# A causal convolution of four taps written as three convolutions of two taps over half the columns

## The chip, the cores and the metric

The kernel runs on one core of one Trainium2 chip. The metric is the device time in microseconds from the first to the last instruction of that core. The engines are named as in the profile: PE is TensorE, DVE is VectorE, ACT is ScalarE, POOL is GpSimd and SP is SyncE, which here only issues DMAs. PSUM is the memory that PE writes, in eight banks of 512 float32 columns.

## The reference

A state-space block and a feed-forward block with selected tokens, each followed by a layer norm. The input is `x`, four batches of 512 tokens of 256 channels, all float32. The first block, cut to what matters here:

```python
xz = x @ W_in
xc, r = jnp.split(xz, 2, axis=-1)
xt = xc.transpose(0, 2, 1)
xconv = lax.conv_general_dilated(xt, conv_w, (1,), [(3, 0)])     # 4 taps, 256 -> 256 channels, causal
xs = (xconv + conv_b[None, :, None]).transpose(0, 2, 1)
u = silu(xs)
dbc = u @ W_x
delta = softplus(dbc[..., :dtr] @ W_dt + b_dt)                   # then B and C from dbc
# scan over 512 tokens: h = exp(delta * A) * h + delta * u * B;  y = sum over 16 states of h * C
out = (y + u * D) * silu(r)
return out @ W_out + xs                                          # x + this goes into the layer norm
```

The second block picks 64 tokens of each batch by a router score, runs attention and a gated MLP over these 256 tokens, puts them back, and a last layer norm follows.

## The kernel before

Channels lie on the 128 partitions (two halves, `o` or `i` = 0, 1) and the 512 tokens of one batch along the free dimension. `W_in` is multiplied into the taps at the start, on PE, so that the convolution reads `x` itself: `conv_x[k, i]` holds the weights of tap k for input half i. `xT` is the transposed `x` of one batch with three zero columns (`PAD`) ahead.

Each engine has a program written out by hand; they meet only in semaphores. The work of a batch is cut into pieces, and the lists `FRONT_AT` (L42), `TAIL_AT` (L53), `FIRST_FRONT` (L49) and `EARLY` (L51) say at which step each engine issues its part of a piece. The main loop has 64 steps t, 16 for each batch b, each with two scans:

- DVE: `scan(2t)`, `scan(2t+1)` (L1179), each over 128 x 512, which write `state`; then its parts of the pieces of step t.
- PE: `turn_bu(2t+2)`, `add_states(t-3)`, the tail pieces, `turn_bu(2t+3)`, the front pieces. `turn_bu(u)` (L651) transposes a quarter of `zed` into the bank that scan u reads, four banks in turn, so it waits for scan u-4. `add_states` (L668) folds the weighed states into a bank.
- ACT: `make_decay(2t+2)`, `make_decay(2t+3)` (L1030; each needs scan u-4 done), in even steps six instructions of `make_z` (L1016), then tail and front pieces.
- POOL: `weigh(t-1)` (L1557), the rest of `make_z`, and other pieces.

Pieces of batch b run ahead of its scans: `xT0`, `xT1` (PE transposes, ACT copies them out of PSUM into `xT`) at step 16b-24, the convolution quarters `cv0a` to `cv0d` at 16b-23 to 16b-20 and `cv1a` to `cv1d` at 16b-19 to 16b-16, `su` (ACT: silu of the convolution) at 16b-13. For batch 2 these are steps 8, 9 to 16 and 19, for batch 3 steps 24, 25 to 32 and 35. Batch 0 does all of them ahead of the loop. Batch 1 does `xT` to `cv1a` ahead of the loop (list `EARLY`, with `du0`, `du1` of batch 0 after `cv0b`, `turn_bu(0)` after `cv0c`, `turn_bu(1)` after `cv0d`), and `cv1b` to `cv1d` at steps 0 to 2.

`convolve(b, o, quarter)` (L542) is one quarter of the convolution for output half o: two matmuls of 128 x 128 weights over 512 columns. Eight of them, for four taps and two input halves, add up in one bank. In the trace a float32 matmul of the program is two MATMUL records. When the last quarter is filled, ACT copies the bank with the bias added into `xsT` (L929).

The front pieces share PSUM banks 6 and 7 in turn: `add_rest` (L115) gives them out in the order of the program, and a convolution holds its bank from `cv?a` to `cv?d` (`held`). `wait_free(pe, name)` makes PE wait until the bank's last contents are drained.

In the list ahead of the loop, DVE is free until the softplus of batch 0 (piece `s3`, L1199), whose two halves end in `delta` and `duT`; SP then spreads `delta` by eight DMAs for the first decays. In steps 10 and 11 DVE has `s4`, `s5` and `s6` of batch 1 (L1217, L1224, L1229); for later batches POOL does `s5` and `s6`.

## Time and profile before

| | us |
|---|---|
| median of three runs | 477.36 (476.84 to 479.91) |
| the profiled execution | 478.12 |
| its span, first to last instruction | 476.4 |

The profile is one execution. Spans and starts below are microseconds from its first instruction. Engines work side by side, so a change is worth what the engine that others wait for gains at that place. The first scan starts at about 61 us and the last step of the loop ends at about 335 us; all that is changed lies between 20 and 211 us.

### The profile page before, as it was taken

Reading aid. Unit: us, or ns where it says so; the run is one execution under the profiler, and the core shown is the slowest. Engines: PE = TensorE matmul, PEld = TensorE weight load, DVE = VectorE, ACT = ScalarE, POOL = GpSimd, SP = SyncE. Lnnn points to the kernel's source line nnn. Section 1 sums busy time; section 2 is a strip of 40 time slices with the busy share of each in tenths; the row PEclk is TensorE's granted clock in tenths of the full one; section 3 lists DMA queues with packets and bytes.
Section 4 is the critical chain, followed back from the end, with each engine's and each line's share of the span. In section 5 each row is a group of like instructions: output and inputs, shape, how many; then the busy total and the mean of one; then the engine's idle time right before and its main releaser. Section 6 shows DMA issues by size and latency. Waiting matters only on the chain. (4 is left out here: it accounts for less than half of the span.)

```text
span 476.4 us, 6481 instructions
## 1 busy us (share of the span) xinstructions
PE 413.1 (87%) x2037; PEld 250.5 (53%) x2037; DVE 302.2 (63%) x604; ACT 294.5 (62%) x628; POOL 278.7 (59%) x245
## 2 busy tenths in 40 slices
PE   4997899889999989999978789768978998999991
PEld 3442453344446435545434456333666877888880
DVE  0400665479683568965659977999488596554355
ACT  4325688796777795678699576963262556543152
POOL 2001056859888859979778999977653254331022
PEclk9998999999999979999988899979997999999996
DMA  6100611004310000510000514870400000000013
GB/s 231 48 6 14 164 48 45 22 23 97 106 45 23 21 23 14 142 46 24 23 22 3 124 55 146 274 287 2 178 0 2 0 1 1 3 1 0 1 53 123
DMA packets 18710, 29.10 MB, mean 61 GB/s; under 512 B 2699, under 2 KB 10677, under 8 KB 18421
## 3 DMA queue, kind: packets, MB, share of 16 engines
q1 hardware_dynamic: 18676, 28.70, 19.4%
q8 instruction: 16, 0.26, 0.2%
q14 instruction: 18, 0.14, 0.1%
HBM read 22.27 MB, written 2.23 MB: 51 GB/s over the span
## 5 line engine op out<-in xcount | busy, mean ns | idle before, releaser
L1186 DVE TENSOR_TENSOR_SCAN state<-front_a,bank 128x512 f32<-128x512 f32 x88 | 102.9, 1206 | 43.8 <-PE bank L538 22.0
L538 PEld LDWEIGHTS bank<-ident,loop_buf 128*128 128x128 f32 x512 | 60.4, 146 | 82.1 <-issue 37.7
L538 PE MATMUL bank<-ident,loop_buf 128*128 128x128 f32 x512 | 85.0, 291 | 16.2 <-ACT loop_buf L1027 14.6
L1037 ACT ACTIVATE front_a<-loop_buf,a_neg 128x512 f32<-128x512 f32 x128 | 84.2, 711 | 7.8 <-DVE copy L1186 4.6
L1027 ACT ACTIVATE loop_buf<-copy,b_rows 128x256 f32<-128x256 f32 x190 | 78.9, 495 | 0.1
L554 PE MATMUL bank<-front_c,conv_raw 128*128 128x512 f32 x128 | 60.7, 607 | 2.5 <-ACT front_c L902 0.9
L1186 DVE TENSOR_TENSOR_SCAN copy<-front_a,bank 128x512 f32<-128x512 f32 x40 | 47.0, 1208 | 23.5 <-PE bank L538 8.1
L1563 POOL TENSOR_TENSOR state<-state,front_a 128x1024 f32<-128x1024 f32 x22 | 52.5, 2387 | 6.1 <-DVE state L1186 6.0
L1563 POOL TENSOR_TENSOR state<-state,c_own 128x1024 f32<-128x1024 f32 x22 | 52.7, 2396 | 4.2 <-DVE state L1186 3.9
L675 PE MATMUL bank<-state,fold 128*64 128x512 f32 x176 | 51.2, 661 | 0.8 <-POOL state L1563 0.8
L1576 POOL TENSOR_TENSOR loop_buf<-copy,b_rows 128x512 f32<-128x512 f32 x31 | 33.6, 1084 | 24.5 <-ACT copy L902 21.9
L554 PEld LDWEIGHTS bank<-front_c,conv_raw 128*128 128x128 f32 x128 | 23.0, 195 | 22.9 <-issue 20.8
L1592 POOL TENSOR_TENSOR loop_buf<-state 128x256 f32<-128x256 f32 x24 | 17.9, 746 | 27.2 <-DVE state L1332 27.2
L1536 POOL TENSOR_TENSOR copy<-front_c,front_b 128x1024 f32<-128x1024 f32 x4 | 8.0, 2003 | 38.0 <-ACT front_b L902 33.1
L902 ACT ACTIVATE front_b<-bank,vec 128x512 f32<-128x512 f32 x16 | 10.9, 683 | 29.4 <-PE bank L554 26.3
L902 ACT ACTIVATE copy<-bank 128x512 f32<-128x512 f32 x20 | 11.7, 595 | 25.7 <-PE bank L538 15.6
L1563 POOL TENSOR_TENSOR copy<-copy,front_a 128x1024 f32<-128x1024 f32 x10 | 24.6, 2465 | 2.7 <-DVE copy L1186 2.7
L699 PE MATMUL bank<-h,copy 128*128 128x128 f32 x192 | 24.4, 283 | 1.4 <-ACT h L1044 0.9
L1563 POOL TENSOR_TENSOR copy<-copy,c_own 128x1024 f32<-128x1024 f32 x10 | 23.9, 2391 | 2.6 <-DVE copy L1186 2.6
L699 PEld LDWEIGHTS bank<-h,copy 128*128 128x128 f32 x192 | 23.0, 196 | 4.3 <-issue 3.0
L675 PE MATMUL bank<-copy,fold 128*64 128x512 f32 x80 | 22.5, 641 | 0.4 <-POOL copy L1563 0.4
L1204 DVE TENSOR_SCALAR front_c<-front_b 128x512 f32<-128x512 f32 x2 | 0.9, 430 | 30.3 <-ACT front_b L966 30.3
(202 smaller groups left out, 740.1 us busy)
## 6 DMA issues: line engine op xcount, KB each, us to landing
front_a<-c_stage SPq DMA_DIRECT2D x32, 128.0 KB, 2.9
c_own<-c_stage SPq DMA_DIRECT2D x32, 128.0 KB, 2.8
loop_buf<-front_b SPq DMA_DIRECT2D x32, 128.0 KB, 2.3
copy<-in_L_attn_x SPq DMA_DIRECT2D x4, 512.0 KB, 3.8
front_b<-in_L_ffn_wo SPq DMA_DIRECT2D x1, 2048.0 KB, 10.9
copy<-in_L_ffn_wq SPq DMA_DIRECT2D x1, 2048.0 KB, 8.0
out<-loop_buf SPq DMA_DIRECT2D x3, 512.0 KB, 3.0
conv_raw<-in_L_attn_conv_w SPq DMA_DIRECT2D x2, 512.0 KB, 4.2
```

Source lines behind the costliest of these rows:

```text
L538: return pe.transpose(dst, src, ident[:])
L554: mm = pe.matmul(at(name)[:], conv_x[:, k, i, o * P:(o + 1) * P], xT[:, i, k:k + L], start=(j == 0), stop=(j == TAPS * KD - 1))
L675: mm = pe.matmul(bank[Y_BANK[h]][j * P // 2:(j + 1) * P // 2, :], fold[:], state[t % NH][:, j, :], start=(m == 0), stop=(m == NPAIR - 1))
L699: mm = pe.matmul(at(name)[:, i * P:(i + 1) * P], w_qk[:, k, head * P:(head + 1) * P], hT[:, k, p * P:(p + 1) * P], start=(k == 0), stop=(k ...
L902: drain_done(name, act.activation(dst, at(name)[:] if src is None else src, func, **kw))
L1027: act.activation(zed[:, g % NZ, c, :, i, :], du_rows[b % 2][:, c, :].rearrange("p (k d) -> p k d", k=2 * KD), ACT.Copy, scale=b_rows[:, b ...
L1037: act.activation(decay[:, u % NDA, :], delta_wide[:, b % 2, k, :], ACT.Exp, scale=a_neg[:, k, m:m + 1]).then_inc(decay_made, 1)
L1186: dve.tensor_tensor_scan(state[t % NH][:, j, :], decay[:, u % NDA, :], bank[BU_BANK[u % NBU]][:], 0.0, ALU.mult, ALU.add).then_inc(scanned, 1)
L1536: pool.tensor_tensor(resT[b % 2], xT[:, :, PAD:], xsT, ALU.add).then_inc(res_ready, 1)
L1563: pool.tensor_tensor(state[t % NH], state[t % NH], c_wide[g % NCW].unsqueeze(1).to_broadcast([P, 2, L]), ALU.mult).then_inc(weighed, 1)
L1576: pool.tensor_tensor(zed[:, g % NZ, c], rows, cols, ALU.mult).then_inc(z_pool, 1)
L1592: pool.tensor_tensor(qkT[:, 2 * j:2 * j + 2, p * P:(p + 1) * P], qk_raw[:, i0 % NQK], qk_swap[:, i0 % NQK], ALU.add).then_inc(roped, 1)
```

## The change

The four-tap convolution of one output half becomes three parts, each of two taps over every second column. With even outputs y0 and odd outputs y1, A = the even taps over the even shifts, B = the odd taps over the odd shifts, S = the sums of neighbouring taps over the sums of neighbouring columns:

- part a (`even0`, `even1`): four matmuls of 257 columns, `conv_x[0]` and `conv_x[2]` over `xT` read with a step of two elements, into a bank of its own. ACT copies it out into `even_buf`.
- part b: four matmuls of 256 columns, taps 1 and 3, again with a step of two, into the first half of the bank of `cv0` or `cv1`.
- part c: four matmuls of 256 or 255 columns, `tap_sum` over `x_pair`, into the second half of that bank.
- part d: nothing on PE. DVE puts the outputs together in three instructions.

DVE also makes `x_pair` from the bank of `xT0` and `xT1`, after ACT has copied from it, and the bank is free only then. DVE makes `tap_sum` once. The bank of even0 comes out of the same turn as the others. ACT no longer copies the convolution out, and at the start of the loop it has `cv1a` of batch 1 where it had `cv0d`. `even_buf` and `odd_part` lie in the buffer of `gT`, `tap_sum` in that of `h`, `x_pair` in that of `change`.

```diff
             if piece[:2] == "cv":
                 if piece[-1] == "a":
+                    add_rest(("even" + piece[2], b))
+                elif piece[-1] == "b":
                     held[0] = add_rest((piece[:3], b))
...
-            def convolve(b, o, quarter):
-
-                name = (f"cv{o}", b)
-                if quarter == 0:
+            def convolve(b, o, part):
+
+                out = slice(o * P, (o + 1) * P)
+                wait_drained(pe, ("xT0", b))
+                wait_drained(pe, ("xT1", b))
+                if part == "a":
+                    name = (f"even{o}", b)
                     wait_free(pe, name)
...
+                        mm = pe.matmul(at(name)[:, 0:HALF + 1], conv_x[:, 2 * m, i, out], xT[:, i, 2 * m:2 * m + L + 1:2],
+                                       start=(j == 0), stop=(j == 2 * KD - 1))
+                    fill_done(name, mm)
+                elif part == "b":
+                    name = (f"cv{o}", b)
+                    wait_free(pe, name)
...
+                        mm = pe.matmul(at(name)[:, 0:HALF], conv_x[:, 2 * m + 1, i, out], xT[:, i, 2 * m + 1:2 * m + L:2],
+                                       start=(j == 0), stop=(j == 2 * KD - 1))
+                elif part == "c":
+                    name = (f"cv{o}", b)
                     if b == 0:
...
+                        pe.wait_ge(taps_added, 4)
+                    for i in range(KD):
+                        mm = pe.matmul(at(name)[:, HALF:], tap_sum[:, 1, i, out], x_pair[:, i, :],
+                                       start=(i == 0), stop=(i == KD - 1), skip_group_check=True)
+                    for i in range(KD):
+                        mm = pe.matmul(at(name)[:, HALF + 1:], tap_sum[:, 0, i, out], x_pair[:, i, 0:HALF - 1],
+                                       start=False, stop=True, skip_group_check=True)
                     fill_done(name, mm)
...
-                    copy_out(name, xT[:, o, PAD:])
+                    wait_filled(act, name)
+                    act.activation(xT[:, o, PAD:], at(name)[:], ACT.Copy).then_inc(x_copied, 1)
...
-                elif piece in ("cv0d", "cv1d"):
+                elif piece in ("cv0a", "cv1a"):
...
-                    copy_out((piece[:3], b), xsT[:, o, :], func=ACT.Identity, bias=vec[:, CB + o:CB + o + 1])
+                        wait_drained(act, (f"cv{o}", b - 1))
+                    copy_out((f"even{o}", b), even_buf[:, o, :], at((f"even{o}", b))[:, 0:HALF + 1])
...
+            front(1, "cv0a")
             front(0, "du0")
             front(0, "du1")
             make_z(0, 0)
...
             make_decay(0)
             make_decay(1)
-            front(1, "cv0d")
+            front(1, "cv1a")
...
+            def add_taps():
+
+                for v in range(4):
+                    j, k = v // 2, 2 * (v % 2)
+                    wait_drained(dve, ("vc", v))
+                    dve.tensor_tensor(tap_sum[:, k // 2, j, :], conv_x[:, k, j, :], conv_x[:, k + 1, j, :],
+                                      ALU.add).then_inc(taps_added, 1)
+
             def front(b, piece):
-                if piece == "s3" and b == 0:
+                if piece in ("xT0", "xT1"):
+                    o = int(piece[-1])
+                    dve.wait_ge(x_copied, KD * b + o + 1)
+                    drain_done((piece, b), dve.tensor_reduce(x_pair[:, o, :], at((piece, b))[:].rearrange("p (s e) -> p s e", e=2),
+                                                             AX.X, ALU.add))
+                elif piece in ("cv0d", "cv1d"):
+                    o = int(piece[2])
+                    name, t = (f"cv{o}", b), at((f"cv{o}", b))
+                    wait_drained(dve, (f"even{o}", b))
+                    wait_filled(dve, name)
...
+                    dve.scalar_tensor_tensor(out=cols[:, 0], in0=t[:, 0:HALF], scalar=shift_by, in1=even_buf[:, o, 0:HALF],
+                                             op0=ALU.add, op1=ALU.add)
+                    link(dve.tensor_tensor(odd_part, t[:, 0:HALF], even_buf[:, o, 1:], ALU.add))
+                    drain_done(name, dve.scalar_tensor_tensor(out=cols[:, 1], in0=t[:, HALF:], scalar=shift_by, in1=odd_part,
+                                                              op0=ALU.add, op1=ALU.subtract))
...
+                    for piece in ("xT0", "xT1"):
+                        front(1, piece)
                     for h in range(KD):
                         dve.wait_ge(sp_log, h + 1)
...
+            add_taps()
             for piece in FIRST_FRONT:
                 front(0, piece)
...
                 scan(2 * t)
                 scan(2 * t + 1)
+                if t == 0:
+                    front(1, "cv0d")
```

## Rows read from the trace of the kernel before

**Rows 1.** The page, busy time of each engine, share of the span, instructions.

```profile
PE 413.1 (87%) x2037; PEld 250.5 (53%) x2037; DVE 302.2 (63%) x604; ACT 294.5 (62%) x628; POOL 278.7 (59%) x245
```

**Rows 2.** Timeline (start, duration, instructions, idle before), ahead of the loop.

```profile
21.12 0.60 ACT L902 ACTIVATE front_c<-bank 128x512 f32<-128x512 f32 x1 [0.26 <-PE bank L538]
21.92 13.97 PE L554 MATMUL bank<-front_c,conv_raw 128*128 128x512 f32 x32 [0.84 <-issue]
35.93 0.69 ACT L902 ACTIVATE front_b<-bank,vec 128x512 f32<-128x512 f32 x1 [3.47 <-PE bank L554]
36.65 1.06 ACT L938 ACTIVATE copy<-front_b 128x1024 f32<-128x1024 f32 x1
37.85 3.65 PE L582 MATMUL bank<-copy,w_x_s 128*128 128x512 f32 x4 [1.96 <-ACT copy L938]
```

**Rows 3.** Timeline of PE: one quarter in steps 12 and 25, and 257-column matmuls.

```profile
114.38 1.88 PE L554 MATMUL bank<-front_c,conv_raw 128*128 128x512 f32 x4
174.84 3.41 PE L554 MATMUL bank<-front_c,conv_raw 128*128 128x512 f32 x4
201.90 1.90 PE L641 MATMUL bank<-x,onehot 128*64 128x257 f32 x8
```

**Rows 4.** Groups of PE instructions: transposes (busy us, mean ns | idle before).

```profile
L538 PE MATMUL bank<-ident,conv_raw 128*128 128x128 f32 x16 | 3.9, 424 | 4.4 <-DMA conv_raw<-in_L_attn_conv_w 4.4
L538 PE MATMUL bank<-ident,front_a 128*128 128x128 f32 x4 | 1.1, 428 | 1.0 <-DMA front_a<-in_L_attn_W_in 1.0
```

**Rows 5.** Groups of DVE instructions of 256 and 128 columns.

```profile
L1388 DVE TENSOR_REDUCE top<-bank 128x1 f32<-128x256 f32 x16 | 6.6, 415 | 0.0
L1387 DVE TENSOR_REDUCE top<-bank 128x1 f32<-128x128 f32 x16 | 4.7, 291 | 13.8 <-PE bank L799 13.7
L1439 DVE SCALAR_TENSOR_TENSOR change<-bank,gate,state 128x256 f32<-128x256 f32 x2 | 1.0, 484 | 5.2 <-PE bank L859 5.2
L1402 DVE TENSOR_TENSOR state<-bank,sel 128x256 f32<-128x256 f32 x2 | 0.8, 424 | 3.2 <-PE bank L827 3.2
```

**Rows 6.** Groups of ACT instructions: the bias copy, and a copy of 257 columns.

```profile
L902 ACT ACTIVATE front_b<-bank,vec 128x512 f32<-128x512 f32 x16 | 10.9, 683 | 29.4 <-PE bank L554 26.3 <-PE bank L602 3.1
L1010 ACT ACTIVATE sel<-bank 64x257 f32<-64x257 f32 x4 | 1.5, 381 | 14.8 <-PE bank L641 14.8
```

**Rows 7.** Timeline from the softplus of batch 0 to step 3.

```profile
52.33 3.67 PE L554 MATMUL bank<-front_c,conv_raw 128*128 128x512 f32 x8 [0.94 <-ACT front_c L902]
52.70 0.69 DVE L1210 TENSOR_TENSOR front_b<-front_b 128x512 f32<-128x512 f32 x1 [0.55 <-ACT front_b L977]
60.24 1.33 ACT L1037 ACTIVATE front_a<-loop_buf,a_neg 128x512 f32<-128x512 f32 x2 [0.89 <-DMA loop_buf<-front_b]
61.07 2.36 DVE L1186 TENSOR_TENSOR_SCAN state<-front_a,bank 128x512 f32<-128x512 f32 x2 [1.44 <-ACT front_a L1037]
62.12 0.69 ACT L902 ACTIVATE front_b<-bank,vec 128x512 f32<-128x512 f32 x1 [0.54 <-PE bank L554]
72.72 0.69 ACT L902 ACTIVATE front_b<-bank,vec 128x512 f32<-128x512 f32 x1 [1.45 <-PE bank L554]
```

**Rows 8.** Timeline of steps 8 to 14: DVE from the scans of step 8, and ACT.

```profile
94.96 2.33 DVE L1186 TENSOR_TENSOR_SCAN state<-front_a,bank 128x512 f32<-128x512 f32 x2 [3.35 <-issue]
98.28 2.33 DVE L1186 TENSOR_TENSOR_SCAN state<-front_a,bank 128x512 f32<-128x512 f32 x2 [0.99 <-PE bank L538]
101.11 1.05 ACT L902 ACTIVATE front_c<-bank 128x512 f32<-128x512 f32 x2
108.78 3.12 DVE L1224 TENSOR_TENSOR front_b<-front_b 128x1024 f32<-128x1024 f32 x1
115.11 6.76 DVE L1186 TENSOR_TENSOR_SCAN state<-front_a,bank 128x512 f32<-128x512 f32 x6
```

**Rows 9.** Timeline of steps 24 to 32: the same places one batch later.

```profile
168.44 2.33 DVE L1186 TENSOR_TENSOR_SCAN state<-front_a,bank 128x512 f32<-128x512 f32 x2 [0.99 <-PE bank L538]
173.22 1.06 ACT L902 ACTIVATE front_c<-bank 128x512 f32<-128x512 f32 x2
```

More of the change, by code:

```diff
@@ L316, in block_kernel @@
         gT = gT_buf[:].rearrange("p (k l) -> p k l", k=KD)
+        HALF = L // 2
+        even_buf = gT_buf[:, 0:KD * (HALF + 1)].rearrange("p (k s) -> p k s", k=KD)
+        odd_part = gT_buf[:, KD * (HALF + 1):KD * (HALF + 1) + HALF]
         z = sb("z", [P, C, DM])
@@ L333, in block_kernel @@
         sel = sb("sel", [P, ST, NCOL])
+        tap_sum = h_buf[:].rearrange("p (m k o) -> p m k o", m=TAPS // 2, k=KD)
+        x_pair = change_buf[:].rearrange("p (k s) -> p k s", k=KD)
         cosT = sb("cosT", [P, S])
@@ L380, in block_kernel @@
         pool_seq = sem("pool_seq")
+        x_copied = sem("x_copied")
+        taps_added = sem("taps_added")
         u_ready = sem("u_ready")
@@ L549, in convolve @@
                     pe.wait_ge(conv_pad, 1)
-                for j in range(2 * quarter, 2 * quarter + 2):
-                    k, i = j // KD, j % KD
-                    if b == 0:
-                        wait_drained(pe, ("vc", 2 * i + k // 2))
-                    mm = pe.matmul(at(name)[:], conv_x[:, k, i, o * P:(o + 1) * P], xT[:, i, k:k + L],
-                                   start=(j == 0), stop=(j == TAPS * KD - 1))
-                if quarter == 3:
+                    for j in range(2 * KD):
+                        m, i = j // KD, j % KD
+                        if b == 0:
+                            wait_drained(pe, ("vc", 2 * i + m))
+                        mm = pe.matmul(at(name)[:, 0:HALF + 1], conv_x[:, 2 * m, i, out], xT[:, i, 2 * m:2 * m + L + 1:2],
+                                       start=(j == 0), stop=(j == 2 * KD - 1))
@@ new lines, in convolve @@
+                    fill_done(name, mm)
+                elif part == "b":
+                    name = (f"cv{o}", b)
+                    wait_free(pe, name)
+                    for j in range(2 * KD):
+                        m, i = j // KD, j % KD
+                        mm = pe.matmul(at(name)[:, 0:HALF], conv_x[:, 2 * m + 1, i, out], xT[:, i, 2 * m + 1:2 * m + L:2],
+                                       start=(j == 0), stop=(j == 2 * KD - 1))
+                elif part == "c":
+                    name = (f"cv{o}", b)
+                    if b == 0:
+                        pe.wait_ge(taps_added, 4)
[5 more added lines that the diff above has]
+                                       start=False, stop=True, skip_group_check=True)
@@ L922, in front @@
                         act.preload_act_table_set("natural_log_exp_and_others")
-                elif piece in ("cv0d", "cv1d"):
+                elif piece in ("cv0a", "cv1a"):
                     o = int(piece[2])
-                    if b == 0 and o == 0:
-                        wait_drained(act, "vec")
                     if b >= 1:
-                        act.wait_ge(res_ready, b)
-                    copy_out((piece[:3], b), xsT[:, o, :], func=ACT.Identity, bias=vec[:, CB + o:CB + o + 1])
+                        wait_drained(act, (f"cv{o}", b - 1))
+                    copy_out((f"even{o}", b), even_buf[:, o, :], at((f"even{o}", b))[:, 0:HALF + 1])
                     if b == 0 and o == 0:
@@ L934, in front @@
                 elif piece == "su":
+                    wait_drained(act, ("cv0", b))
                     wait_drained(act, ("cv1", b))
@@ L1196, in make_z @@
                                       ALU.mult).then_inc(z_dve, 1)
-            def front(b, piece):
-                if piece == "s3" and b == 0:
+            def add_taps():
[4 more added lines that the diff above has]
+                                      ALU.add).then_inc(taps_added, 1)
+            def front(b, piece):
+                if piece in ("xT0", "xT1"):
[8 more added lines that the diff above has]
+                    wait_filled(dve, name)
+                    if b == 0 and o == 0:
+                        wait_drained(dve, "vec")
+                    if b >= 1:
+                        dve.wait_ge(res_ready, b)
+                        dve.wait_ge(u_ready, b)
+                    cols = xsT[:, o, :].rearrange("p (s e) -> p e s", e=2)
+                    shift_by = vec[:, CB + o:CB + o + 1]
+                    dve.scalar_tensor_tensor(out=cols[:, 0], in0=t[:, 0:HALF], scalar=shift_by, in1=even_buf[:, o, 0:HALF],
[3 more added lines that the diff above has]
+                                                              op0=ALU.add, op1=ALU.subtract))
+                elif piece == "s3" and b == 0:
                     for h in range(KD):
```

4 lines of the change are left out of this document (1 added, 3 removed).

## The prediction

> **What bounds the kernel now.** I read the page's busy times first. PE is busy for 87% of the span, DVE, ACT and POOL for about 60% each [rows 1]. That makes PE the engine to relieve, but it is an average, so I then read the timeline of each engine at the places where the change lies. Ahead of the loop PE works alone: ACT sits idle for 3.47 us until the convolution's last matmul, and the silu follows directly [rows 2]. In the loop the four engines run in a ring: PE's transposes wait for the scan four back, a decay waits for the scan four back, a scan waits for both. Whoever is last in a step sets it. During convolution steps this is mostly PE, but at the start of the loop and around `xT` it is ACT (DVE waited 1.44 us for a decay [rows 7]) or the order of DVE's list.
>
> **What PE loses.** In the program's float32 a quarter is four records of 512 columns: 1.88 us, with the end of the last one, or 13.97/8 = 1.75 us in a row of eight [rows 2, 3]. Eight records of 257 columns took 1.90 us [rows 3], so a part a, b or c costs what a quarter did. Three in place of four take 1.75 us from each of eight half-convolutions: 14 us of PE's work, 3.5 per batch.
>
> Parts a and b read every second column. No row shows whether that costs anything. Lower bound nothing; upper bound twice the time, 1.75 us more for each part. The nearest rows are transposes out of `conv_raw` with a step of four elements in one of the two operands, 424 ns each, beside 428 ns for those with a step of one [rows 4]: equal. I take nothing. The Trainium skill (SBUF — State Buffer, Door 1: The DMA port swizzle) says that SBUF is read in lines of 16 bytes and that a second access to the same line comes at full rate, which for float32 with a step of two would be free. By the same rule a step of four should cost something; the two rows differ by nothing, though they do not tell which operand has the step. The sum is the same by page and rows.
>
> **What DVE gains.** A reduce of 256 columns takes 415 ns and one of 128 takes 291 [rows 5], 0.97 ns a column, so 512 columns are 0.66 us; per batch two, 1.3 us. The three instructions of part d read PSUM and SBUF over 256 columns: 484, 424 and 484 ns [rows 5], 1.4 us per half. DVE gets 4.1 us per batch. The four `tap_sum` adds (about 0.42 each) run while PE still makes the taps, and part c needs them only 3.5 us after the convolution starts: nothing. ACT changes a 683 ns copy for one of 381 [rows 6], 0.6 us less per batch, and no longer waits for the last quarter. Bounds of DVE's share: 0.3 us a half less (if the instructions overlap their ends) to 0.7 us more (beside POOL, where L1224 took 3.12 us for 1024 columns [rows 8]; those two inputs both lie in SBUF, the new ones don't).
>
> **Ahead of the loop.** PE starts when both banks of `xT` are free: ACT's copy ends at 21.72, the reduce at about 22.4, so +0.5. Two quarters less: -3.5. The output is put together in 1.4 us on DVE instead of 0.69 on ACT: +0.7. The silu comes 2.3 us early, at 34.3. PE then waits as before, and its four records of 3.65 us after the pause of 1.96 (0.9 us each instead of 0.44: the lower clock [rows 2]) stay.
>
> **Into the loop.** In `s3` DVE has the two reduces between its two halves. Before the add at 52.70 it had 0.55 us to spare [rows 7], so 1.3 - 0.55 = +0.75, and the decays and the first scan come 1.5 us early, at 59.5. The convolution of batch 1 waited for ACT's copy until 52.33; now it waits for the second reduce.
>
> Now the step that I take as decisive. Counting `add_rest` through the new list puts cv0 of batch 1 in bank 6, du0 in 7 and even1 again in bank 6. So PE's `cv1a` waits until DVE has drained cv0, and DVE does this after both scans of step 0: 59.5 + 2.3 + 1.4 = 63.2. Queued behind `cv1a` on PE are `turn_bu(2)` and (3); behind even1's copy on ACT are decays 2 and 3, so DVE's next scans. Part a ends at 65.0, the copy at 65.5. Before, ACT's copy at this place ended at 62.8 [rows 7]: +2.7. ACT then worked on to its next copy at 72.72, ahead of which it was idle for 1.45 us [rows 7]. The idle time and the copy itself (0.6) are gone, so at step 3 ACT is 0.7 us later than before: the 1.5 us gained are lost and 0.7 more. PE has stood idle for 4 us ahead of part a. After 1.96 us it fell to the lower level [rows 2], and a quarter at that level took 3.41 instead of 1.88 [rows 3]. I expect that here too: +1.6. Sum to step 3: **+2.3** (bounds +0.7 and +2.5; -1.5 if the wait is hidden).
>
> **Batch 2, steps 8 to 17.** DVE is done with step 8 at 97.3, but its reduces stand ahead of step 9 and need ACT's copies, which come at 101.11 to 102.16, after a decay pair and `make_z` [rows 8]. Step 9 scans at 103.0 instead of 98.28: 4.7 us late. From 98.28 to L1224 at 108.78 DVE had three pairs of scans and `s4`, 8.2 of 10.5 us, so 2.3 are absorbed and 2.4 remain. Then `cv0d` adds 1.4 after step 12: the scans that ended at 121.9 [rows 8] end at 125.7. PE loses its quarter at 114.38, but must then wait for the first scan of step 12, to about 118.8: this quarter is traded for idle time. In steps 14 to 16 PE sets the pace again and its missing last quarter gives 1.75 back, against 1.4 for `cv1d` on DVE. ACT, no longer waiting for cv1d, comes to `su` up to 1 us early. That is -1.0 to 0; the 4 us pause of PE adds up to 1.5 by the clock. I take **+0.5**.
>
> **Batch 3, steps 24 to 33.** The same with ACT's copies at 173.22 to 174.3 [rows 9], since `la0` and `la1` stand ahead of them: step 25 scans at 175.1 instead of 168.44, +6.7. PE had its `cv0a` only at 174.84 [rows 3], so it loses just 0.3; POOL has its own waits there. DVE catches up to about +3.3 at step 30, with `cv0d` in it, and two quarters less bring PE back: at step 34 the scans stand at +0.2, ACT at -1 or better, and ACT sets the next steps. **-1.0** (bounds -1.7 and +3.3).
>
> **Sum.** 2.3 + 0.5 - 1.0 = +1.8 us, so the execution of 478.12 becomes 479.9. It lies 0.76 above the median of 477.36; against the median the forecast is 479.2 us, +0.4%. Of 14 us taken from PE nearly all goes into waits. [...]
>
> **The rivals.** *PE's time comes through*, 20%: batch 1's wait is hidden and half of the six quarters in the loop reach the end: -1.5 - 5.2 = -6.7, 470.7 us. For it: PE is busy 87%, and it is idle for little in the convolution steps. Against it: DVE's list around `xT`. *DVE's delays are never given back*, slower, 19%: a scan waits for ACT's `xT` copy with all of DVE behind it. It decides once DVE stays the last engine through steps 14 and 30: +2.3 + 3.8 + 3.3 = +9.4, 486.8 us. Against it: PE is idle then and has less to do. *The step of two costs PE double*, 4%: 7 us more per batch, all of it ahead of the loop and half of it in three batches: +1.8 + 7 + 10.5 = +19, 497 us. Against it: rows 4.
>
> **How the numbers follow.** My forecast has 57% and by its bounds (-1.0, +0.7 and up to +3) runs from 475 to 483. The range reaches from 471 to 487, beyond which lie half of the faster rival, the double read and some of the slow one, together 2 in 10. This kernel's measurement tells about 1%, 4.8 us, from no change. Faster than 472.6: 0.18. Slower than 482.1: 0.26, the slow rivals and the upper end of mine. Between: 0.56.
>
> **What the changed profile would show.** Ahead of the loop: 48 records of 257, 256 and 255 columns about 10.5 us long, silu near 34.3; 17 us or more if the step of two costs. First scan near 59.5. PE idle for about 4 us ahead of the first record of even1, with DVE as releaser, and a lower clock after it; ACT's decay pair after it near 66 to 67. DVE idle from 97 to 102 until ACT's copy, with the scans of step 9 behind it, and from 167 to 174. PE idle for some 4 us near 115. I am wrong in the main step if PE is not idle ahead of even1, and in the sum if step 17 and step 34 begin over 2 us away from where these terms put them.

## The result, and the profile after

The changed kernel took 485.28 us (median of 4 runs, 484.31 to 491.5), the kernel before 478.02 beside it on the same chip (4 runs): a ratio of 1.0168, 95% interval 1.0118 to 1.0218. It is 1.7% slower. The time lies in the range of 471 to 487, but the forecast of 479.2 was 6 us too low. "Within 1%", which had the largest chance, did not come, and the time lies outside the 475 to 483 that the prediction gave to its own case. (Ratios leave out executions in which the chip was disturbed, the medians and ranges here don't, so the two can differ by some tenths of a per cent.)

| | before | after |
|---|---|---|
| median | 478.02 us | 485.28 us |
| profiled execution, its time | 478.12 us | 484.31 us |
| its span | 476.4 us | 482.6 us |
| mean granted clock of TensorE in it | 0.952 | 0.942 |

The page of after, busy times (compare [rows 1]):

```profile
PE 405.5 (84%) x2101; PEld 267.1 (55%) x2101; DVE 316.9 (66%) x640; ACT 292.8 (61%) x628; POOL 278.7 (58%) x245
```

PE is busy 7.6 us less and the span is 6.2 us longer: PE stands idle for about 14 us more than before. Where it does, the groups of lines tell (busy us, mean ns | idle time before them and what ended it); L564 is part a, L1238 the reduce, L1252 to L1255 part d:

```profile
L564 PE MATMUL bank<-front_c,conv_raw 128*128 128x257 f32 x64 | 20.8, 478 | 13.7 <-DVE change L1238 5.4 <-DVE junk L1327 4.8 <-DVE front_b L1255 3.4
L1238 DVE TENSOR_REDUCE change<-bank 128x256 f32<-128x512 f32 x8 | 5.2, 688 | 11.1 <-ACT front_c L941 11.0
L1252 DVE SCALAR_TENSOR_TENSOR front_b<-bank,vec,gT 128x256 f32<-128x256 f32 x8 | 3.8, 473 | 11.0 <-PE bank L582 11.0
L1254 DVE TENSOR_TENSOR gT<-bank,gT 128x256 f32<-128x256 f32 x8 | 3.3, 412 | 0.0
L1255 DVE SCALAR_TENSOR_TENSOR front_b<-bank,vec,gT 128x256 f32<-128x256 f32 x8 | 3.9, 484 | 0.3
```

Of PE's 14 us of new idle time most stands ahead of one line, part a (the convolution's line of before had 2.5 us ahead of it), and each of its three releasers is DVE: 5.4 us for the sums of neighbours, 3.4 us for the bank of `cv0` of batch 1, and 4.8 us for "junk L1327", which the prediction does not mention. DVE itself waits 11.0 us for ACT's copies ahead of the reduces.

The timeline of after ahead of the loop (start, duration, instructions, idle before; compare [rows 2]):

```profile
21.76 2.05 PE L564 MATMUL bank<-front_c,conv_raw 128*128 128x257 f32 x8 [1.46 <-DVE change L1238]
23.65 1.98 PE L572 MATMUL bank<-front_c,conv_raw 128*128 128x256 f32 x8
34.26 1.06 ACT L965 ACTIVATE copy<-front_b 128x1024 f32<-128x1024 f32 x1 [4.67 <-DVE front_b L1255]
35.46 1.95 PE L609 MATMUL bank<-copy,w_x_s 128*128 128x512 f32 x4 [2.74 <-ACT copy L965]
```

The silu starts at 34.26, 2.4 us earlier than before. The four records behind it took 1.95 us, where before they took 3.65, though PE had stood idle for longer (2.74 us, not 1.96).

The way into the loop (compare [rows 7]):

```profile
51.84 3.13 PE L572 MATMUL bank<-front_c,conv_raw 128*128 128x256 f32 x8
59.03 2.33 DVE L1214 TENSOR_TENSOR_SCAN state<-front_a,bank 128x512 f32<-128x512 f32 x2 [0.45 <-PE bank L547]
62.10 0.48 DVE L1255 SCALAR_TENSOR_TENSOR front_b<-bank,vec,gT 128x256 f32<-128x256 f32 x1
62.85 3.76 PE L564 MATMUL bank<-front_c,conv_raw 128*128 128x257 f32 x8 [3.45 <-DVE front_b L1255]
66.71 0.39 ACT L929 ACTIVATE gT<-bank 128x257 f32<-128x257 f32 x1 [7.17 <-PE bank L564]
66.99 1.32 ACT L1064 ACTIVATE front_a<-loop_buf,a_neg 128x512 f32<-128x512 f32 x2
67.80 2.33 DVE L1214 TENSOR_TENSOR_SCAN state<-front_a,bank 128x512 f32<-128x512 f32 x2 [5.21 <-ACT front_a L1064]
```

This is the chain that was forecast: `cv0d` on DVE ends at 62.58, part a of `even1` starts 0.27 us later and takes 3.76 us, then come ACT's copy, the decays, and the scans of step 1 with 5.21 us of idle time ahead of them.

Around `xT` of batches 2 and 3 (steps 9 and 25; compare [rows 8, 9]):

```profile
104.51 1.29 DVE L1238 TENSOR_REDUCE change<-bank 128x256 f32<-128x512 f32 x2 [4.42 <-ACT front_c L941]
105.72 2.32 DVE L1214 TENSOR_TENSOR_SCAN state<-front_a,bank 128x512 f32<-128x512 f32 x2
...
177.62 1.29 DVE L1238 TENSOR_REDUCE change<-bank 128x256 f32<-128x512 f32 x2 [6.38 <-ACT front_c L941]
178.82 2.32 DVE L1214 TENSOR_TENSOR_SCAN state<-front_a,bank 128x512 f32<-128x512 f32 x2
```

And in step 29, with batch 3's `even1`:

```profile
198.59 0.35 DVE L1327 SCALAR_TENSOR_TENSOR junk<-bank,x,earlier 128x128 bf16<-128x128 f32 x1
...
199.21 3.76 PE L564 MATMUL bank<-front_c,conv_raw 128*128 128x257 f32 x8 [4.81 <-DVE junk L1327]
203.07 0.39 ACT L929 ACTIVATE gT<-bank 128x257 f32<-128x257 f32 x1 [9.59 <-PE bank L564]
```

L1327 is the last of the router's rank comparisons. It reads the scores of batch 0 (`sb`) out of bank 7, and the new list of fills puts `even1` of batch 3 in that bank. PE stands idle for 4.81 us, part a then takes 3.76, and ACT had nothing to do for 9.59 us.

The granted clock of these stretches, to be set beside PE's pauses of 3.45 and 4.81 us (the columns: window and its length, busy us of PE, PEld, DVE, ACT and POOL, then the clock as a share of 2.4 GHz, DMA share and GB/s):

```profile
61.00:68.00 7.00, 5.15 (x16) 4.31 (x17) 1.75 (x5) 1.29 (x3) 2.35 (x1) 0.51 0.00 0
197.50:204.30 6.80, 5.09 (x16) 4.17 (x17) 6.61 (x15) 0.82 (x2) 4.35 (x2) 0.51 0.62 147
```

At 0.51 both lie almost wholly at the lower level, 1.2 GHz of 2.4.

Of everything later the starts of the scans tell. The table gives, for each kernel, by how much more (or less, with a minus) it took than before from the span's start to the scan of step 0, from there to that of step 5, and so on; the experiments below are in it too. "(8 to 9)" is a part of "5 to 24", and "(24 to 25)" of "24 to 37". The sum is that up to the scan of step 63; behind it a trace differs from before by up to 1.4 us more. Batch 1 falls in steps 0 to 5, batch 2 in 5 to 24, batch 3 in 24 to 37.

| us against before | to step 0 | 0 to 5 | 5 to 24 | (8 to 9) | 24 to 37 | (24 to 25) | 37 to 63 | sum |
|---|---|---|---|---|---|---|---|---|
| after | -2.0 | +4.8 | +1.0 | +4.6 | +2.4 | +6.6 | 0.0 | +6.2 |
| e1_bank_b1 | -2.7 | -0.8 | -0.6 | +4.6 | +1.2 | +6.6 | +1.1 | -1.8 |
| e2_bank_b3 | -2.2 | +4.8 | +3.8 | +4.6 | -2.5 | +6.6 | -0.4 | +3.5 |
| e3_reduce_late | -3.3 | +4.6 | +2.6 | 0.0 | -1.0 | 0.0 | -0.1 | +2.7 |
| e4_all_three | -1.9 | -0.8 | +1.2 | 0.0 | -1.9 | 0.0 | +3.4 | +0.1 |
| e5_pe_cut_alone | -4.5 | -0.1 | -2.7 | 0.0 | -3.4 | 0.0 | -0.4 | -11.1 |
| e6_reduce_alone | +2.1 | +1.0 | +0.2 | +4.6 | +5.5 | +6.6 | -0.4 | +8.4 |
| e7_contiguous | -3.5 | +4.7 | +2.5 | +4.6 | +2.4 | +6.6 | +1.1 | +7.3 |
| e8_three_act_out | -1.7 | -0.8 | -0.8 | 0.0 | -0.5 | 0.0 | +2.6 | -1.2 |
| e9_pairs_from_sbuf | -5.9 | -1.6 | -0.4 | 0.0 | -3.0 | 0.0 | +3.4 | -7.4 |
| e10_sbuf_even_late | 0.0 | -1.6 | -1.2 | 0.0 | -3.7 | 0.0 | +0.4 | -6.0 |
| e11_sbuf_even_late_again | -3.7 | -1.6 | -1.2 | 0.0 | -3.7 | 0.0 | +2.6 | -7.6 |
| e12_pairs_only | -4.1 | +4.8 | +2.7 | +4.6 | +3.7 | +6.6 | +0.4 | +7.6 |

How far the columns can be trusted: e10 and e11 are one kernel and differ by 3.7 us in the first and 2.2 in "37 to 63", but by 0.1 or less in the others. After and e2 have the same code until step 29, and in "5 to 24" e2 takes 2.8 us more, all of it between the scans of steps 10 and 15, where its clock was lower (see the last section). E7, which differs from after only in which columns PE reads, takes 1.5 us more there. So in "5 to 24" a difference of up to 3 us can be the clock.

### The profile page after: what moved, and what is told of

Its sections match the earlier page's. It is cut to its first block and busy times, and to the rows that moved or that the text cites. A ratio compares the mean times of both kernels' runs of the same rounds, so it can differ in the third digit from the quotient of the medians.

```text
span 482.6 us, 6684 instructions
## 1 busy us (share of the span) xinstructions
PE 405.5 (84%) x2101; PEld 267.1 (55%) x2101; DVE 316.9 (66%) x640; ACT 292.8 (61%) x628; POOL 278.7 (58%) x245
## 5 line engine op out<-in xcount | busy, mean ns | idle before, releaser
L564 PE MATMUL bank<-front_c,conv_raw 128*128 128x257 f32 x64 | 20.8, 478 | 13.7 <-DVE change L1238 5.4
L929 ACT ACTIVATE gT<-bank 128x257 f32<-128x257 f32 (+1 forms) x10 | 4.2, 428 | 33.0 <-PE bank L564 33.0
L929 ACT ACTIVATE copy<-bank 128x512 f32<-128x512 f32 x20 | 11.8, 595 | 20.4 <-PE bank L547 9.7
L564 PEld LDWEIGHTS bank<-front_c,conv_raw 128*128 128x128 f32 x64 | 14.3, 234 | 17.6 <-issue 8.7
L1387 DVE SCALAR_TENSOR_TENSOR state<-bank,vec,cosT 128x128 f32<-128x128 f32 x48 | 14.4, 339 | 7.8 <-ACT state L1087 7.8
```

Source lines behind the costliest of these rows:

```text
L564: mm = pe.matmul(at(name)[:, 0:HALF + 1], conv_x[:, 2 * m, i, out], xT[:, i, 2 * m:2 * m + L + 1:2], start=(j == 0), stop=(j == 2 * KD - 1))
L929: drain_done(name, act.activation(dst, at(name)[:] if src is None else src, func, **kw))
L1387: ins = dve.scalar_tensor_tensor(out=qk_raw[:, i0 % NQK, i, :], in0=at(name)[:, i * P:(i + 1) * P], scalar=vec[:, w:w + 1], in1=cosT[:, to ...
```

## The experiments

The theory after the traces: three waits that the new order of work makes, and not DVE's added work, hold the loss. They are (W1) `even1` of batch 1 in bank 6, which waits for `cv0d`; (W3) `even1` of batch 3 in bank 7, which waits for `sb` of batch 0; (R) the reduces of batches 2 and 3 ahead of the scans of steps 9 and 25, with ACT's copies late. The rivals: DVE's added work by itself; the step of two columns; ACT's and PE's added dependence at large, which would stay when the three are gone.

**e1: W1 undone.** `even1` of batch 1 gets bank 7, and cv1 of batch 1 bank 6:

```diff
+    FORCED = {("even1", 1): 7}
...
+                    if (piece[:3], b) == ("cv1", 1):
+                        fills.add(("cv1", 1), 6)
+                        held[0] = 6
```

> The changed kernel with one edit: even1 of batch 1 goes to bank 7 (last used by du0, drained by ACT early) and cv1 of batch 1 to bank 6, so that PE's cv1a ahead of the loop no longer waits for DVE's cv0d behind the two scans of step 0. Theory W (three waits make the loss, this is one): part a of even1 starts near 59.5 us instead of 62.85 and at the full clock, ACT's copy of it comes near 61.5 instead of 66.7, the scans of step 5 start at 80 instead of 83.84, and the kernel takes 3 to 4 us less than the changed one, 481 to 482. Rival D (the 4 us of added DVE work per batch are the loss wherever they stand): under 1 us less, 484 to 485. Rival P (the half-wide matmuls with a step of two cost PE more than the rows say): no change here.

Measured: 479.96 us (10 runs, 472.73 to 488.1) against 478.0 (29 runs, 474.35 to 484.12; the same beside e2 to e4), ratio 0.9963 (0.9914 to 1.0012). PE's timeline:

```profile
58.33 1.99 PE L574 MATMUL bank<-front_c,conv_raw 128*128 128x257 f32 x8
...
62.09 2.06 PE L582 MATMUL bank<-front_c,conv_raw 128*128 128x256 f32 x8 [0.90 <-DVE front_b L1265]
```

Part a of `even1` now runs at 58.33 without a wait, in 1.99 us; the wait has moved to part b and shrunk to 0.90. From step 0 to step 5 the kernel takes 0.8 us less than before, where after took 4.8 more: W1 costs 5.6 us of the trace between these steps. The medians lie 5.3 us apart (485.28 to 479.96), the ratios 2.05% or 9.8 us; with executions that spread over 15 us, the trace is the better measure.

**e2: W3 undone.** `even1` of batch 3 in bank 6, and du0 and du1 of batch 2, which had it, too:

```diff
+    FORCED = {("even1", 3): 6, ("du0", 2): 6, ("du1", 2): 6}
```

> The changed kernel with one edit: even1 of batch 3, and du0 and du1 of batch 2 behind it, go to bank 6 instead of 7, 6 and 7. Bank 7 holds the scores (piece sb) of batch 0 until DVE's k3 at step 29, for which PE waited 4.8 us ahead of even1. Theory W: PE starts this part a near 194.5 instead of 199.2 and without the lower clock, the one-hot of step 30 comes 4 us earlier, the scans of step 31 start at 205 instead of 208.9, and the kernel takes 2.5 to 4 us less, 481 to 483. Rival D: DVE is the last engine in steps 26 to 33 anyway, under 1 us less. Rival P: no change.

Measured: 482.05 us (10 runs, 479.58 to 486.69), ratio 1.0103 (1.0061 to 1.0145).

```profile
197.47 2.05 PE L572 MATMUL bank<-front_c,conv_raw 128*128 128x257 f32 x8 [0.44 <-DVE front_b L1263]
```

The pause of 4.81 us is one of 0.44, the part takes 2.05 us, and steps 24 to 37 take 2.5 us less than before instead of 2.4 more: 5.0 us. The median shows 3.2 of them. (In the trace 2.8 go the other way, between the scans of steps 10 and 15, ahead of the first fill that e2 moves.)

**e3: R undone.** DVE does its reduces of batches 2 and 3 one step later, behind the scans:

```diff
-                for b, piece in fronts(t):
-                    front(b, piece)
+                for b, piece in fronts(t - 1) + fronts(t):
+                    if piece in ("xT0", "xT1"):
+                        if (b, piece) in fronts(t - 1):
+                            front(b, piece)
+                    elif (b, piece) in fronts(t):
+                        front(b, piece)
```

> The changed kernel with one edit: for batches 2 and 3 DVE makes its two reduces of xT one step later in its list, behind the scans of steps 9 and 25 instead of ahead of them, so that these scans no longer wait for ACT's copy of xT. Theory W: the scans of step 9 start near 101 instead of 105.7 and those of step 25 near 172 instead of 178.8; part of this is absorbed before, so 1.5 to 4 us less in all, 481.5 to 484. Rival D: the same DVE work, the same time within 0.5 us.

Measured: 483.7 us (4 runs, 480.76 to 487.58), ratio 1.0147 (1.0084 to 1.0209). DVE's timeline at step 9:

```profile
99.61 2.33 DVE L1214 TENSOR_TENSOR_SCAN state<-front_a,bank 128x512 f32<-128x512 f32 x2 [0.99 <-PE bank L547]
103.04 1.29 DVE L1238 TENSOR_REDUCE change<-bank 128x256 f32<-128x512 f32 x2 [1.10 <-ACT front_c L941]
```

The scan is no longer behind the reduce, and both jumps of the table (4.6 and 6.6 us) are gone. Batch 2 is no shorter for it, though (5 to 24: +2.6, after +1.0): there the jump had been given back anyway, as forecast. In batch 3 it is worth 3.4 us of the trace (-1.0 against +2.4). The median is 1.6 us lower, which the intervals do not tell from nothing.

**e4: all three undone.** The edits of e1, e2 and e3 together.

> The changed kernel with the edits of the three runs before this one together. Theory W: their gains add up to 7 to 10 us, and what PE was spared shows: 475 to 478, level with the kernel before or up to 3 us faster. Rival D: 482 to 485, slower than before by 1%.

Measured: 476.95 us (12 runs, 473.88 to 481.22), ratio 0.9969 (0.9936 to 1.0002). The three are worth 8.3 us of the median (9.5 by the ratios). This is less than the sum of their single gains (5.3 + 3.2 + 1.6 = 10.1): W3 and R lie in the same batch, and in steps 24 to 37 they gave 5.0 and 3.4 us alone but 4.3 together. What is left is a kernel level with before, with 14 us less work for PE: so the waits explain the loss, but not why there is no gain.

**e5: PE's cut alone.** The kernel before with its last quarter left out of every half-convolution. It computes a convolution of three taps; it shows what 14 us less of PE are worth when nothing is added for them.

```diff
-                for j in range(2 * quarter, 2 * quarter + 2):
+                for j in range(2 * quarter, 2 * quarter + 2) if quarter < 3 else ():
```

> The kernel before with the last tap left out: quarters cv0d and cv1d hold no matmuls and the bank counts as filled after cv0c and cv1c. So PE is spared the same 1.7 us per half, 14 in all, and nothing is added on any engine. Its output is not the reference's, since one of four taps is missing. Theory W (PE's time is worth something by itself, and the added waits took it): 3.4 us ahead of the loop, 1.5 to 2 in batch 1's steps 0 to 2, 1.5 to 2.5 in each of batches 2 and 3, so 467 to 471 against 478. Rival L (in the loop another engine sets the step, so that only the part ahead of the loop counts): 474 to 475.

Measured: 467.62 us (4 runs, 466.77 to 470.62) against 477.14, ratio 0.9826 (0.9783 to 0.987).

```profile
19.52 10.54 PE L554 MATMUL bank<-front_c,conv_raw 128*128 128x512 f32 x24 [0.84 <-issue]
```

The cut is worth 9.5 us, two thirds of its 14: about 3.4 ahead of the loop (10.54 for 13.97 [rows 2]), nothing in batch 1 (-0.1), 2.7 in batch 2 and 3.4 in batch 3, where all of PE's time comes through. From 467.62 to 485.28 lie 17.7 us, the price of what the change adds.

**e6: the reduces alone.** The kernel before with DVE's reduces of both `xT` banks, which must be done before the banks are free, and with nothing that uses them. (So its `xT` still feeds four taps.)

```diff
-                    copy_out(name, xT[:, o, PAD:])
+                    wait_filled(act, name)
+                    act.activation(xT[:, o, PAD:], at(name)[:], ACT.Copy).then_inc(x_copied, 1)
```

> The kernel before with only DVE's two reduces of xT per batch and their waits, at the places of the changed kernel (x_pair is made and not used; the convolution is as before). Theory W: 0.6 us later ahead of the convolution, 0.7 at the softplus, the scans of step 9 at 103 to 105 and those of step 25 4 to 7 us after their place before, of which about half is absorbed: 481 to 484. Rival D (the reduces cost their own time, 5 us of DVE in all, mostly beside other work): 478 to 480.

Measured: 488.87 us (4 runs, 485.93 to 491.36) against 477.14, ratio 1.0259 (1.0209 to 1.0309). More than expected. DVE's timeline:

```profile
104.84 1.29 DVE L1205 TENSOR_REDUCE change<-bank 128x256 f32<-128x512 f32 x2 [4.42 <-ACT front_c L916]
...
177.17 1.29 DVE L1205 TENSOR_REDUCE change<-bank 128x256 f32<-128x512 f32 x2 [6.38 <-ACT front_c L916]
178.38 2.32 DVE L1189 TENSOR_TENSOR_SCAN state<-front_a,bank 128x512 f32<-128x512 f32 x2
```

These are the waits of after, to the hundredth (4.42, 6.38), so they owe nothing to the convolution. DVE works 5 us more; the kernel loses 11.7. In batch 2 the jump is given back (5 to 24: +0.2), in batch 3 it isn't (+5.5). PE has its full convolution there and may lack the time to catch up; that was not tested. What is added for 5 us of DVE's work costs more than PE's cut is worth.

**e7: the step of two.** The changed kernel with parts a and b reading 257 and 256 neighbouring columns. It computes another thing; the work is the same in number and size.

```diff
-                        mm = pe.matmul(at(name)[:, 0:HALF + 1], conv_x[:, 2 * m, i, out], xT[:, i, 2 * m:2 * m + L + 1:2],
+                        mm = pe.matmul(at(name)[:, 0:HALF + 1], conv_x[:, 2 * m, i, out], xT[:, i, 2 * m:2 * m + HALF + 1],
```

> The changed kernel with parts a and b reading as many columns with a step of one instead of two. Its output is not the reference's, since the wrong columns go into these products. In the changed kernel's trace ahead of the loop part a took 1.89 us, part b 1.82 and part c, with a step of one, 1.72. Theory S (the step of two costs PE 5 to 10%): a and b fall to 1.72 each, 2 us of PE's work less in all, 0 to 1.5 us in the kernel's time. Rival (what differs between the parts is the start of a new group of weights or of a bank): a and b stay at 1.82 to 1.89.

Measured: 486.14 us (4 runs, 485.7 to 487.03), ratio 1.0206 (1.0171 to 1.0241), no faster than after.

```profile
21.92 1.97 PE L564 MATMUL bank<-front_c,conv_raw 128*128 128x257 f32 x8 [1.46 <-DVE change L1238]
23.73 1.89 PE L572 MATMUL bank<-front_c,conv_raw 128*128 128x256 f32 x8
25.46 1.03 PE L579 MATMUL bank<-change,h 128*128 128x256 f32 x4
```

From part a's start to part b's are 1.81 us (21.92 to 23.73), in after 1.89 (21.76 to 23.65); the records took 1.97 and 1.89 here, 2.05 and 1.98 there. The step of two costs 0.08 to 0.09 us a part in this place, 4%, some 1.3 us of PE over the 16 parts, and nothing of the time. That rival has fallen.

**e8: e4 without part d.** e4 with DVE's three instructions replaced by ACT's one copy with the bias, as before; the even part is not added, so the output lacks it.

```diff
-                    cols = xsT[:, o, :].rearrange("p (s e) -> p e s", e=2)
...
+                    copy_out((piece[:3], b), xsT[:, o, :], func=ACT.Identity, bias=vec[:, CB + o:CB + o + 1])
```

> The kernel of e4_all_three with DVE's three instructions of part d left out: ACT copies the bank of cv0 and cv1 with the bias into the rows, as the kernel before does, in the places of the kernel before. Its output is not the reference's, since the even part is not added. DVE has 11 us less work. Theory W (with the three waits gone DVE's own added work costs little): 1 to 3 us less than e4, 474 to 476. Rival D (the added DVE work is what still eats PE's gain): 5 us less or more, 472 or below.

Measured: 475.42 us (12 runs, 472.38 to 481.33), ratio 0.9961 (0.9927 to 0.9995), 1.5 us below e4 by the medians; e4 was timed in another set, so by the ratios it is 0.4 us. With the waits gone, 11 us of DVE's work for part d (against ACT's copies, which come back in its place) cost 0.4 to 1.5 us. DVE's added work by itself is not the price.

**e9: the bank freed by ACT alone.** e4 with the sums made from the copy `xT` in SBUF. ACT's copy frees the banks of xT0 and xT1 as it did before, and PE waits for the sums only ahead of part c:

```diff
-                    wait_filled(act, name)
-                    act.activation(xT[:, o, PAD:], at(name)[:], ACT.Copy).then_inc(x_copied, 1)
+                    copy_out(name, xT[:, o, PAD:])
...
+                    pe.wait_ge(x_added, KD * (b + 1))
...
+                    wait_drained(dve, (piece, b))
+                    dve.tensor_reduce(x_pair[:, o, :], xT[:, o, PAD:].rearrange("p (s e) -> p s e", e=2),
+                                      AX.X, ALU.add).then_inc(x_added, 1)
```

> e4 (the three waits gone) with one more edit: VectorE makes x_pair from the copy xT in SBUF instead of from the PSUM bank, so ScalarE's copy alone drains the banks of xT0 and xT1, and TensorE waits for x_pair only ahead of part c. The theory that what is left above 467.6 + VectorE's and ScalarE's added work is waiting for the sums: 474 to 476, with TensorE's part a of batches 1 to 3 starting about 1 us earlier against e4. The rival (those waits had already gone with e4, TensorE is held by other things): 477, as e4.

Measured: 474.77 us (12 runs, 471.8 to 480.17) against 478.24, ratio 0.9925 (0.9888 to 0.9962). The medians are 2.2 us below e4's, but the two intervals overlap. In the three columns from 0 to 37 it takes 3.5 us less than e4 (0.8, 1.6 and 1.1). The 0.8 came again in e10 and e11; the 1.6 can be the clock. In the first column, 4.0 us less, 3.2 stand ahead of all that differs (the sixteen records of the last section end at 17.2 here and at 20.4 in e4) and 0.7 are PE's wait for the sums.

**e10 and e11: and ACT's even copy one step later.** e9, with ACT's copy of `even0` for batches 2 and 3 behind the decays of the next step:

```diff
-                for b, piece in fronts(t):
-                    front(b, piece)
+                for b, piece in fronts(t - 1):
+                    if piece == "cv0a":
+                        front(b, piece)
+                for b, piece in fronts(t):
+                    if piece != "cv0a":
+                        front(b, piece)
```

> e9 with ScalarE's copy of the even part of half 0 (batches 2 and 3) issued one step later, behind the decays of the next step. If ScalarE's wait for TensorE's part a (683 ns of matmuls and more behind the transposes) holds up the next step's exponentials, 1 to 2 us go: 473 to 475. If ScalarE has slack there, as e9.

Measured: 473.65 us (6 runs, 466.32 to 474.89) against 478.24 (475.79 to 482.49). The six lay wide apart, so the kernel ran once more:

> e10's kernel unchanged, with more executions, since six of it lay between 466 and 475. If e10 stands for the kernel: 472 to 474, below the kernel before by 0.8 to 1.2%. If e10's six were lucky: as e9, 474 to 475.

Measured: 470.2 us (6 runs, 466.95 to 475.5) against 477.42, ratio 0.9834 (0.9774 to 0.9893). All twelve have a median of 471.7, the 28 of before beside them one of 477.5: 1.2% less. Both intervals (e10's ratio is 0.9808, 0.9754 to 0.9862) lie below 1, so this version beats both kernels. From the 467.62 of e5 to 471.7 some 4 us are left that no run takes apart. PE's group of part a in e11:

```profile
L577 PE MATMUL bank<-front_c,conv_raw 128*128 128x257 f32 x64 | 16.4, 397 | 2.5 <-ACT front_c L943 2.5
```

Of 13.7 us of idle time ahead of part a 2.5 are left, none of it with DVE as releaser (ahead of part b, which had none in after, stand 2.7 us now, 1.7 of them for DVE), and the records take 397 ns, not 478, 16.4 us in all for 20.8: what is gone is the lower clock behind the pauses.

**e12: e9's edit alone.** The changed kernel with e9's edit and nothing else.

> The changed kernel with one edit, e9's: x_pair from xT in SBUF, the banks of xT0 and xT1 drained by ScalarE alone, TensorE's wait for x_pair ahead of part c. The bank waits of even1 and the place of the sums ahead of the scans stay. If the three waits undone in e4 are the cost: about what e9 gained on e4, 2 us, from 485.3 to 483. If TensorE's wait ahead of part a was a large one by itself: 480 or less.

Measured: 487.28 us (4 runs, 486.75 to 490.72) against 477.42, ratio 1.0228 (1.0175 to 1.0281). Both expectations were wrong: it is no better than after. By the medians it is 2 us worse, which the intervals do not separate. The two bank waits are there as before:

```profile
60.83 3.76 PE L564 MATMUL bank<-front_c,conv_raw 128*128 128x257 f32 x8 [4.47 <-DVE front_b L1255]
...
200.64 3.76 PE L564 MATMUL bank<-front_c,conv_raw 128*128 128x257 f32 x8 [3.58 <-DVE junk L1327]
```

What PE gains ahead of part a of `even1` in batch 1 becomes a longer wait there, 4.47 us for 3.45, and steps 0 to 5 take the same +4.8. That is shown. Batches 2 and 3 take 1.7 and 1.3 us more than in after. In batch 2 e7, with the code of after, takes as much (+2.5 for +2.7); in batch 3 the granted clock of 190 to 210 us was 0.74, against 0.83 in after. So the clock alone can do it, but that it did isn't shown.

## Why the prediction was off

The chain into the loop and the two jumps were forecast rightly, and the sum failed in batch 3, at a bank wait that it did not contain. That the range held is in part luck: its upper end stood for delays that are never given back, and that is not how the time was lost.

**Ahead of the loop: right, and one row was read as a rule.** The silu was forecast for 34.3 and came at 34.26, though the 48 records took 11.0 us, not 10.5; the reduces took 688 ns each (0.66 by the sum), part d 473 + 412 + 484 ns = 1.37 us (1.4). The first scan was forecast for 59.5 and came at 59.03. But the four records behind the silu, which were to stay at the lower clock, ran at the full one (1.95 us for 3.65), and the convolution of batch 1, a little later, ran partly at the lower (3.13 us for part b). The two nearly cancel. That PE falls after such a pause was taken from one execution; the last section counts the other traces.

**Into the loop, forecast +2.3: right in mechanism, near in size.** PE is idle ahead of `even1` (3.45 us, forecast 4) with DVE's part d as releaser, part a runs at the lower clock, and ACT's decays start at 66.99 (66 to 67). The lower clock cost part a 1.8 us (3.76 for the 1.99 of e1; the term was 1.6, by its own rows 1.5). The sum was given for step 3, with +2.5 as its upper bound: there the scans stood at +4.4, and at +2.8 by step 5, so 1.6 us were given back two steps later than the text had it. e1 shows that it was this bank: 5.6 us go with it. This was the decisive step of batch 1, as the text said.

**Batch 2, forecast +0.5: the jump and its return right, the sum near by luck.** Step 9 comes 4.6 us later against step 8 (4.7), and up to step 24 the batch costs +1.0. But e2 costs +3.8 there with the same code and e7 +2.5, so no single trace tells the sum closer than 3 us. That the jump is given back was argued from DVE's and PE's slack. E3 and e7 show it, for in both the lower clock falls at 102.3 to 105.7 and 122.8 to 126.2 us: without the jump (e3) the batch costs +2.6, with it (e7) +2.5. In e6, the jump alone, it costs +0.2. PE's pause "near 115" came, at 118.84, shorter than the 4 us of the text, and with the clock's fall behind it:

```profile
121.62 0.63 PE L547 MATMUL bank<-ident,loop_buf 128*128 128x128 f32 x4 [2.78 <-DVE state L1214]
...
124.67 2.59 PE L564 MATMUL bank<-front_c,conv_raw 128*128 128x257 f32 x8
```

 At step 17, where the text said it would be judged, the terms put the scan at +2.8 and it stood at +7.2: wrong by the test that was set. It stood at +4.7 one step later and at +3.8 by step 21, so the giving back came later than forecast.

**Batch 3, forecast -1.0: wrong, and this is the miss.** It was +2.4. The step that failed is "two quarters less bring PE back: at step 34 the scans stand at +0.2". Up to step 30 the batch went as forecast or better: the jump at step 25 was +6.6 (forecast +6.7), and at step 30 the batch stood at +2.4 (+3.3). Then, where 3.1 us were to be given back, 1.0 were lost, because PE waited 4.81 us for bank 7 and went on at half its clock. The text had counted the new list of fills for batch 1, but not asked the same question of batch 3: in what bank is each new fill, and who frees it, when? With batch 3's `even1` in bank 6 (e2) steps 24 to 37 take 2.5 us less than before, beyond the lower bound of -1.7. At step 34, the second place where the sum was to be judged, the scan stood at +7.1 for about +3. So 5.0 us of the trace are this one omission, and 3.4 of them are the whole distance between the forecast of batch 3 and what it took. The "slow" rival (DVE's delays never given back, 486.8) had nearly the right time by another road: DVE gave the jump back, in batch 2 fully.

**The size of PE's worth.** The first rival, "PE's time comes through", put its worth at -6.7; by e5 it is -9.5, and 3.4 of 3.5 us in batch 3. That rival was not far from true of PE and wrong of the kernel, for the same three waits stood against it; in the kernel of e10 and e11 they are gone, and its time is near the rival's (471.7, forecast 470.7), though with two more edits and not by the rival's sum.

**The step of two costs PE double: no.** 0.08 to 0.09 us of 1.9 per part, not 1.75 more. Taking nothing was near enough, and the two transposes of [rows 4] were a fair proxy. The rule of the Trainium skill (SBUF — State Buffer, Door 1: The DMA port swizzle) that was weighed there makes a step of two free for float32; the runs show 4% for it.

**DVE's added work.** By e8 part d costs 0.4 to 1.5 us in all once the three waits are gone: DVE had room for it. In the forecast its work stood in the terms of every batch (1.4 each); what counted was what it was the releaser of.

## What to carry to other kernels

When a change puts one more user on a ring of buffers, every later user shifts to another buffer: go through the whole ring, not the first place where it hurts, and ask of each new pair who frees the buffer, and in which step. When an engine takes over a part of another's work, look at what its instruction stands ahead of and what it releases, before looking at how long it takes: here 5 us of reduces cost 11.7 (e6) and 11 us of part d at most 1.5 (e8). Let one engine free a scarce buffer, and let the second reader work from the copy.

## What the runs showed of the hardware

**The clock falls after some pauses and not after others of the same length.** In before PE was idle for 1.96 us ahead of the four records behind the silu, and they ran at the lower level (3.65 us); in after it was idle for 2.74 us at the same place and they ran at the full one (1.95 us). Ten traces have this pause at 2.74 or 2.75 us. In seven of them the four records took 1.95 or 1.96 us, in e2, e10 and e11 they took 3.42 to 3.65:

```profile
37.16 3.65 PE L623 MATMUL bank<-copy,w_x_s 128*128 128x512 f32 x4 [2.74 <-ACT copy L978]
```

That is e10. Yet each of the eight pauses of 3.4 to 4.8 us ahead of part a was followed by 3.56 to 3.77 us for it. The Trainium skill (TensorE: Matmul & The Clock Gate, What's actually happening) says that the gate judges how busy the engine has been, over stretches that run on their own, whatever the kernel does. By that one pause could fall either way, and these rows agree. After and e2 show it over the same code, in windows from 96 to 140 us (the clock is the third number from the end), first after:

```profile
96.00:112.00 16.00, 13.72 (x74) 8.07 (x72) 9.82 (x10) 13.67 (x25) 7.58 (x6) 1.00 0.06 17
112.00:126.00 14.00, 10.50 (x47) 6.05 (x48) 13.87 (x12) 7.29 (x15) 13.79 (x6) 0.88 0.47 115
126.00:140.00 14.00, 13.67 (x75) 8.42 (x74) 10.29 (x11) 11.98 (x24) 10.83 (x6) 1.00 0.21 63
```

```profile
96.00:112.00 16.00, 13.79 (x69) 8.38 (x68) 9.24 (x10) 12.31 (x22) 6.12 (x5) 0.89 0.06 17
112.00:126.00 14.00, 10.22 (x46) 5.24 (x44) 12.99 (x11) 8.64 (x18) 13.92 (x7) 0.86 0.39 90
126.00:140.00 14.00, 13.68 (x69) 9.49 (x68) 9.24 (x10) 9.85 (x21) 9.52 (x6) 0.90 0.26 84
```

The second is e2, which lost its 2.8 us here. Later, where no edit is near, e4's trace has a longer low stretch than before's:

```profile
262.00:276.00 14.00, 12.46 (x51) 7.62 (x52) 10.69 (x9) 6.30 (x13) 14.00 (x8) 0.63 0.48 126
```

```profile
262.00:276.00 14.00, 11.03 (x60) 6.62 (x57) 12.55 (x23) 6.42 (x13) 13.87 (x7) 0.88 0.49 121
```

The first is e4, the second the kernel before; e4 loses 3.4 us between steps 37 and 63. Four traces (e4, e8, e9, e11) have a low stretch of about 10 us in this part, the others none above 7, and that column is +2.6 to +3.4 in them; in all others it is -0.4 to +1.1. The clock is also part of why 29 executions of one kernel lie between 474.4 and 484.1: the three with the highest mean clock (0.965 and 0.968) are the three fastest. It isn't all, for the slowest had 0.952, as had one of 479.67 us.

**The start of the program varies too.** L783 in e9 and e10 is the same work of sixteen records ahead of the convolution, in the same code:

```profile
10.09 7.11 PE L783 MATMUL bank<-front_a 128*128 128x512 f32 x16
```

```profile
11.77 9.59 PE L783 MATMUL bank<-front_a 128*128 128x512 f32 x16
```

In e9 it starts at 10.09 and takes 7.11 us, in e10 at 11.77 and 9.59: 4.2 us between two profiles before anything that either edit touches. Against a term of 2 us a single pair of profiles says nothing there; between steps 0 and 37 two traces can be compared to some tenths where their clocks fall in the same places, as in e10 and e11, and to 3 us where they don't.
